# Sparse attention with a threshold search: new guess and steps, measures over two items, a fourth buffer

## The reference

```python
scores = einsum('bhqd,bhkd->bhqk', qh, kh) * scale
attn = sparsemax(scores)          # clip(scores - tau, 0), tau such that each row sums to 1
out = einsum('bhqk,bhkd->bhqd', attn, vh)
```

## Time and profile before

| | us |
|---|---|
| median of 3 runs (6928.72 to 6942.44) | 6930.95 |
| the profiled execution | 6886.64 |
| its span | 6884.8 |
| DVE busy in the span | 6013.5 |
| ACT busy in the span | 5560.1 |
| PE busy in the span | 5091.3 |
| POOL busy in the span | 2476.3 |

### The profile page before, as it was taken

One profiled execution on the slowest core, in us unless ns is written; L12 is line 12 of the kernel. 1 busy time (PEld: TensorE's weight loads), 2 busy tenths in 40 slices (PEclk: granted clock), 3 DMA queues, 4 the chain that ended last, 5 costly groups with the idle time before them and its releaser, 6 DMA issues. The chain is left out here.

```text
span 6884.8 us, 164804 instructions
## 1 busy us (share of the span) xinstructions
PE 5091.3 (74%) x19554; PEld 1665.0 (24%) x19555; DVE 6013.5 (87%) x50066; ACT 5560.1 (81%) x12484; POOL 2476.3 (36%) x10299
## 2 busy tenths in 40 slices
PE   8985777776777777676777777777777777758794
PEld 5551111111111111111111111111111111127573
DVE  4558999999999999999999999999999999958545
ACT  3336998998999999898999999998999999953231
POOL 2222333333333333333333333333333333325431
PEclk9996676766676666666666666666766766778897
DMA  5762111111111111111111111111111111136335
GB/s 195 238 200 59 30 33 30 31 33 30 31 32 32 31 31 32 28 31 27 31 31 32 31 31 31 32 31 29 34 32 32 31 33 34 31 126 240 96 100 192
DMA packets 691616, 415.98 MB, mean 60 GB/s; under 512 B 503713, under 2 KB 597537, under 8 KB 690209
## 3 DMA queue, kind: packets, MB, share of 16 engines
q1 hardware_dynamic: 677408, 370.58, 21.6%
q0 software_dynamic: 13056, 35.74, 1.4%
HBM read 249.13 MB, written 156.88 MB: 59 GB/s over the span
## 5 line engine op out<-in xcount | busy, mean ns | idle before, releaser
L887 DVE MAX8 a_cand<-a_scores 128x8 f32<-128x42 f32 (+1 forms) x38912 | 4400.3, 202 | 176.7 <-issue 136.7
L633 ACT ACTIVATE a_junk_act<-a_cand,a_ntau 128x304 f32<-128x304 f32 (+1 forms) x3840 | 1933.4, 522 | 143.6 <-POOL a_ntau L964 50.4
L603 PE MATMUL a_ring<-a_q,a_k 99*128 99x512 bf16 (+1 forms) x3328 | 1469.9, 556 | 735.2 <-ACT a_scores L669 509.2
L548 PE MATMUL a_out<-a_attn,a_v 128*32 128x512 f32 (+1 forms) x6656 | 1401.4, 780 | 543.5 <-ACT a_attn L673 543.5
L669 ACT COPY a_scores<-a_ring 128x1024 f32<-128x1024 f32 (+1 forms) x2048 | 1611.2, 830 | 152.3 <-PE a_ring L599 83.9
L673 ACT ACTIVATE a_attn<-a_ring 128x1024 f32<-128x1024 f32 (+1 forms) x1792 | 1654.2, 975 | 54.4 <-PE a_ring L603 53.3
L599 PE MATMUL a_ring<-a_k,a_q 96*128 96x512 bf16 (+1 forms) x4096 | 1368.7, 464 | 69.7 <-DVE a_ident L700 33.7
L633 ACT ACTIVATION_READ_ACCUMULATOR a_junk_act<-a_cand,a_ntau 128x1 f32 x3840 | 797.6, 208 | 0.0
L599 PEld LDWEIGHTS a_ring<-a_k,a_q 96*128 96x128 bf16 x4096 | 389.8, 117 | 1423.2 <-issue 645.6
L603 PEld LDWEIGHTS a_ring<-a_q,a_k 99*128 99x128 bf16 (+1 forms) x3328 | 287.8, 119 | 1583.2 <-ACT a_scores L669 890.0
L548 PEld LDWEIGHTS a_out<-a_attn,a_v 128*32 128x32 f32 (+1 forms) x6656 | 172.5, 121 | 1200.8 <-ACT a_attn L673 745.5
(11 more groups left out here) (228 smaller groups left out, 6364.8 us busy)
## 6 DMA issues: line engine op xcount, KB each, us to landing
a_k<-k_parts SPq DMA_DIRECT2D x1536, 50.0 KB
k_parts<-p_ks SPq DMA_DIRECT2D x48, 800.5 KB, 7.3
o_parts<-a_o SPq DMA_DIRECT2D x512, 64.0 KB, 1.6
e_o<-o_parts SPq DMA_DIRECT2D x64, 512.0 KB, 7.4
p_ctx<-in_ctx_t SPq DMA_DIRECT2D x16, 1601.0 KB, 8.5
v_heads<-p_v SPq DMA_DIRECT2D x16, 1536.0 KB
a_q<-q_parts SPq DMA_DIRECT2D x1536, 16.0 KB
a_v<-v_heads SPq DMA_DIRECT2D x256, 96.0 KB
```

Source lines behind the costliest of these rows:

```text
L548: mm = nc.tensor.matmul(out_ps[at:at + 2 * HEAD_DIM], beside, attn[0:rows, k, (c % 2) * BANK:(c % 2 + 1) * BANK], start=first and c < 4, s ...
L603: mm = nc.tensor.matmul(at[0:rows, m * BANK:(m + 1) * BANK], k_st[0:SCORE_ROWS + TAU_ROWS, ut, c * P:c * P + rows], q_st[0:SCORE_ROWS + TA ...
L633: ins = nc.scalar.activation(into[:, t].rearrange("p (a b) -> p a b", b=CHUNKS), cand[:, u % SLOTS, t, 0:w], ACT.Relu, bias=ntau[:, u % 2, ...
L887: ins = V.max(cand[:, u % SLOTS, t, :, c], scores[:, u % SLOTS, t, lo:hi])
```

## The change

- **Guess.** DVE's `start` makes `bn_stats` (means and spreads) of the chunks' greatest scores instead, adds the two halves' spreads, and reduces the eighth candidates. POOL's new `guess` makes tau and a model of how tau falls with the excess from these, with one `pow` for a square root. The sums, the counts and their reciprocals are gone from DVE.
- **Round 0** reads six candidates of each chunk (228 per row) instead of four.
- **Steps.** POOL's `first`, then `factors` and `improve` for each of two further steps, replace `second`, `third` and `slope`. Each `factors` needs a reciprocal that DVE makes in `inverse`: one beside t3, one beside t0.
- **Places.** On ACT in step i: after the first group round 2 of item i-2, then round 0 of item i-1, round 3 of item i-2, round 1 of item i-1. DVE's part of round 3 moves from t0 to t2. POOL's order becomes `improve` 1 of item i-2, `guess(i-1)`, `factors` and `improve` 2 of item i-2, `divide_up(i-3)`, `first(i-1)`, `factors` 0 of item i-1, `last_step(i-2)`.
- **An item later.** `settle(i-3)` stands beside t1, `SLOTS` is 4 and `LAG` is 4.
- `BEFORE_LAST` is 4.5e-4 instead of 3e-4; `full_excess` combines its 128 flags with two maxima in place of four copies.

```diff
-FIRST, SECOND = 2, 4
-USUAL_COUNT = 22.0
+SECOND = 6
+GUESS_AT, GUESS_SPREAD = 0.0202, 6.42
+FALL_AT, FALL_SPREAD = 0.0035, 0.693
+NEAR = 0.03, 0.001
-BEFORE_LAST = 3e-4
+BEFORE_LAST = 4.5e-4
...
-    SLOTS = 3
+    SLOTS = 4
-    LAG = 3
+    LAG = 4
+    TAUS = 3
...
-                    if part == 2 and has(i, 2):
-                        count_bad(i - 2)
+                    if part == 0 and has(i, 3):
+                        count_bad(i - 3)
...
-                    if g == 0 and has(i, 2):
-                        measure_excess(i - 2, (u - 2) % U, ROUNDS - 1)
-                    if g > 0 and has(i, 1):
-                        measure_excess(i - 1, (u - 1) % U, g - 1)
+                    if g % 2 == 0 and has(i, 2):
+                        measure_excess(i - 2, (n - 2) % LONG, 2 + g // 2)
+                    if g % 2 == 1 and has(i, 1):
+                        measure_excess(i - 1, (n - 1) % LONG, g // 2)
...
+                c, st = cand[:, u % SLOTS], stats[:, u % 2]
+                for t in range(TILES):
+                    ins = V.bn_stats(st[:, t], c[:, t, 0])
                 yield from link(ins)
+                V.tensor_tensor(spread_sq[:, u % 2], st[:, :, 2], st[:, :, 5], ALU.add).then_inc(spread_made, 1)
+                V.tensor_reduce(tops[:, u % TAUS], c[:, :, 7], AX.X, ALU.max, negate=True)
+
+            def inverse(i, n):
+
+                dve.wait_ge(square_made[n], i + 1)
+                V.reciprocal(square_inv[:], square[:]).then_inc(inv_made[n], 1)
...
+                    if t == 0 and has(i, 1):
+
+                        dve.wait_ge(cand_made, i)
+                        yield from start(i - 1, prev, link)
                     if t == 0 and has(i, 2):
+                        for _ in range(4):
                             yield
+                        inverse(i - 2, 1)
+                    if t == 1 and has(i, 3):
+                        yield from settle(i - 3, done, link)
+                    if t == 2 and has(i, 2):
+                        yield
+                        dve.wait_ge(tau_tried[ROUNDS - 2], i - 1)
...
                     if t == 3 and has(i, 1):
+                        inverse(i - 1, 0)
...
+                def guess(i, u):
+
+                    st, nt = stats[:, u % 2], ntau[:, u % TAUS]
+                    pool.wait_ge(spread_made, i + 1)
                     pool.sem_inc(passed_pool, 1)
+                    G.tensor_tensor(center[:], st[:, :, 1], st[:, :, 4], ALU.add)
+                    link(G.tensor_scalar(near[:], spread_sq[:, u % 2], -GUESS_SPREAD / CHUNKS, GUESS_AT, ALU.mult, ALU.add))
+                    link(G.tensor_scalar(center[:], center[:], -0.5, None, ALU.mult))
+                    G.tensor_tensor(nt, center[:], near[:], ALU.add).then_inc(guessed, 1)
+                    link(G.tensor_tensor(spread[:], spread_sq[:, u % 2], halves[:], ALU.pow))
+                    G.tensor_scalar(fall0[:], spread[:], FALL_SPREAD / CHUNKS ** 0.5, FALL_AT, ALU.mult, ALU.add)
+
+                def first(i, u):
+
+                    nt = ntau[:, u % TAUS]
+                    pool.wait_ge(excess_made[0], i + 1)
                     pool.sem_inc(passed_pool, 1)
+                    link(G.tensor_scalar(over[:], excess[:, u % 2, 0], 2.0, -1.0, ALU.min, ALU.add))
+                    link(G.tensor_scalar(bend[:], over[:], -0.5, 1.0, ALU.mult, ALU.add))
+                    link(G.tensor_tensor(rise[:], over[:], bend[:], ALU.mult))
+                    link(G.tensor_tensor(move[:], rise[:], fall0[:], ALU.mult))
+                    G.tensor_tensor(nt, nt, move[:], ALU.subtract).then_inc(tau_tried[0], 1)
+                    link(G.tensor_tensor(square[:], rise[:], rise[:], ALU.mult))
+                    G.tensor_scalar(square[:], square[:], NEAR[0] ** 2, None, ALU.add).then_inc(square_made[0], 1)
+
+                def factors(i, u, n, fall, rise):
+
+                    G.tensor_scalar(half[:], fall, -0.5, None, ALU.mult)
+                    pool.wait_ge(inv_made[n], i + 1)
                     pool.sem_inc(passed_pool, 1)
+                    link(G.tensor_tensor(share[:], rise, square_inv[:], ALU.mult))
+                    link(G.tensor_tensor(linear[:], share[:], fall, ALU.mult))
+                    link(G.tensor_tensor(cubic[:], linear[:], share[:], ALU.mult))
+                    G.tensor_tensor(linear_b[:, n], linear[:], half[:], ALU.add)
+                    G.tensor_tensor(cubic_b[:, n], cubic[:], linear[:], ALU.subtract)
+
+                def improve(i, u, r, fall, next_fall, over):
+
+                    nt = ntau[:, u % TAUS]
+                    pool.wait_ge(excess_made[r], i + 1)
                     pool.sem_inc(passed_pool, 1)
+                    link(G.tensor_scalar(over[:], excess[:, u % 2, r], 1.5, -1.0, ALU.min, ALU.add))
+                    link(G.tensor_tensor(term[:], over[:], cubic_b[:, r - 1], ALU.mult))
+                    link(G.tensor_tensor(term[:], term[:], linear_b[:, r - 1], ALU.add))
+                    link(G.tensor_tensor(term[:], term[:], over[:], ALU.mult))
+                    link(G.tensor_tensor(next_fall, term[:], fall, ALU.add))
+                    link(G.tensor_tensor(move[:], over[:], next_fall, ALU.mult))
+                    G.tensor_tensor(nt, nt, move[:], ALU.subtract).then_inc(tau_tried[r], 1)
...
+                prev, last = (u - 1) % LONG, (u - 2) % LONG
                 if has(i, 2):
+                    improve(i - 2, last, 1, fall0[:], fall1[:], over1)
+                    link(G.tensor_tensor(square[:], over1[:], over1[:], ALU.mult))
+                    G.tensor_scalar(square[:], square[:], NEAR[1] ** 2, None, ALU.add).then_inc(square_made[1], 1)
                 if has(i, 1):
+                    guess(i - 1, prev)
                 if has(i, 2):
+                    factors(i - 2, last, 1, fall1[:], over1[:])
+                    improve(i - 2, last, 2, fall1[:], fall2[:], over)
+                if has(i, 3):
+                    divide_up(i - 3, (u - 3) % LONG)
                 if has(i, 1):
+                    first(i - 1, prev)
+                    factors(i - 1, prev, 0, fall0[:], rise[:])
+                if has(i, 2):
+                    last_step(i - 2, last)
```

More of the change, by code:

```diff
@@ L433, in attend_program @@
         ones = sb("ones", [P, 1], BF16)
-        ntau = sb("ntau", [P, 2, TILES])
-        tops = sb("tops", [P, 2, 2, TILES])
+        ntau = sb("ntau", [P, TAUS, TILES])
+        tops = sb("tops", [P, TAUS, TILES])
         excess = sb("excess", [P, 2, ROUNDS, TILES])
[L438 to L444, removed]
+        stats = sb("stats", [P, 2, TILES, 6])
+        spread_sq, spread = sb("spread_sq", [P, 2, TILES]), sb("spread", [P, TILES])
+        halves = sb("halves", [P, TILES])
+        center, near = sb("center", [P, TILES]), sb("near", [P, TILES])
+        over, over1, bend, rise, move = (sb(n, [P, TILES]) for n in ("over", "over1", "bend", "rise", "move"))
+        square, square_inv, share = (sb(n, [P, TILES]) for n in ("square", "square_inv", "share"))
+        half, linear, cubic, term = (sb(n, [P, TILES]) for n in ("half", "linear", "cubic", "term"))
+        linear_b, cubic_b = sb("linear_b", [P, 2, TILES]), sb("cubic_b", [P, 2, TILES])
+        fall0, fall1, fall2 = (sb(n, [P, TILES]) for n in ("fall0", "fall1", "fall2"))
         cut_off, far_off = sb("cut_off", [P, TILES]), sb("far_off", [P, TILES])
-        e_bound = sb("e_bound", [P, TILES])
-        square = sb("square", [P, TILES])
-        fall = sb("fall", [P, TILES])
         bad = sb("bad", [P, TILES], BF16)
@@ L668, in step @@
                             t, lo, hi = S_PIECES[m]
-                            nc.scalar.copy(scores[:, u % SLOTS, t, lo:hi], at[:, 0:hi - lo]).then_inc(piece_used, 1)
+                            nc.scalar.copy(scores[:, n % SLOTS, t, lo:hi], at[:, 0:hi - lo]).then_inc(piece_used, 1)
                         else:
@@ L870, in beside @@
                         yield from start(i - 1, prev, link)
-                    if t == 2 and has(i, 2):
-                        yield from settle(i - 2, last, link)
+                    if t == 0 and has(i, 2):
+                        for _ in range(4):
[3 more added lines that the diff above has]
+                        yield from settle(i - 3, done, link)
+                    if t == 2 and has(i, 2):
+                        yield
+                        dve.wait_ge(tau_tried[ROUNDS - 2], i - 1)
+                        for n in range(ACT_LAST, TILES):
+                            values, nt = cand[:, last % SLOTS, n], ntau[:, last % TAUS]
+                            V.scalar_tensor_tensor(out=view(junk, values, CAND, n), in0=values, scalar=nt[:, n:n + 1], in1=zeros_like(values), op0=ALU.add, op1=ALU.max,
+                                                   accum_out=excess[:, last % 2, ROUNDS - 1, n:n + 1]).then_inc(last_summed, 1)
+                            yield
                     if t == 3 and has(i, 1):
-                        for _ in range(5):
```

(3 more changed lines are left out.)

173 lines of the change are left out of this document (46 added, 127 removed).

## The result

The changed kernel takes 7354.82 us (median of 4 runs, 7354.24 to 7361.58), the kernel before beside it 6936.32 (4 runs): ratio 1.0609, 95% interval 1.0596 to 1.0622. Slower, as forecast, but by 418 us instead of 56, outside the range of 6860 to 7090. The profiled execution took 7355.2 us with a span of 7353.3.

The account below looks back on a forecast made before the run. ACT was taken as the bound (97.8% busy in calm stretches), DVE just behind. Calm items +92, flags -41 and draining +5 gave +56 us on 6884.8, 0.8%, scaled to 6987 us; range 6860 to 7090, chance 0.8.

Parts of the forecast that it names:

- How many flags: Tiles sent to the whole-row pass: kept at 41, `cut_off` being unchanged; gain 41 x 1.0 = 41 us.
- floor of 36: Tiles with eight or more keys above tau in one chunk, counted from the reference's inputs: at least 36 stay flagged.
- The search is less exact: Rival on the search for tau: doubled flags cost 41 x 4.4 = 180 us more, 7167 us; chance 0.04.
- The price of a flag: Delay per tile needing the whole-row pass on DVE: 5.4 us before, 4.4 us after the change.
- absorbed: POOL's `divide_up(i-3)`, queued behind the whole-row pass, has 5 us until `first` must follow, so its delay costs nothing.
- The calm item: An item in a stretch without whole-row passes: 20.74 us before, 21.1 after, 0.36 x 256 = 92 us lost.
- term for the chain: From t3's copy over DVE and POOL to round 2: 7.4 us, with ACT's 13.75 a loop of 21.15 against 20.95.
- the wider round 0: ACT's round 0 goes from 152 to 228 elements per row: 0.06 us per tile, 0.25 us per item more.
- busy share: DVE's busy share of the span, 87% before, falls towards 85%; its work per item from 20.0 to 17.6 us.
- `pow`: POOL's square root in the guess: taken as 0.4 us; slow-`pow` rival, above 2.3 us DVE waits, 7090 to 7170, chance 0.12.
- The 5 us for the drain: `LAG` 4 adds a step of draining at the end, less what the first four steps lack: 5 us lost.

Follow-up runs that it names:

- `a_cutonly`: Changed kernel with the last measure's limit out of reach, so that only `cut_off` flags tiles: 7036.27 us, 36 flagged tiles.
- the reorder: Changed kernel with POOL's `last_step(i-2)` put ahead of `factors` 0: 7118.74 us; the same with no tile ever flagged: 6726.44 us.
- `a_divide`: Changed kernel with POOL's `divide_up(i-3)` put behind `first(i-1)`: 7362.4 us.
- `a_noflags`: Changed kernel with both limits out of reach, so that no tile is ever flagged: 6887.42 us.
- `b_noflags`: Kernel before, with both limits out of reach, so that no tile is ever flagged: 6705.71 us.

## Why the prediction went wrong

**The step that failed is "How many flags".** It kept 41, since `cut_off` is unchanged; that gives a floor of 36, and `a_cutonly` shows just 36. The runs count 71. For the tiles beyond the floor nothing in the trace of before speaks: how exact the new guess and steps are is arithmetic, and the prediction set its own rival "The search is less exact" at 0.04. 35 tiles missed by over the limit instead of five. Worked out on the reference's inputs, the excess sum misses 1 in the median by 0.034, 0.0004 and 0.000007 in the first three rounds of the old search, and by 0.064, 0.0035 and 0.00009 in the new: a poorer start and weaker steps. It takes the reference's inputs alone to see that, as for the floor of 36.

**The rival's price was also short.** It doubled the flags at 4.4 us and had no term for further steps: 25 instead of 4, 7.65 us each, cost more (161 us) than the 30 added tiles (117).

**The price of a flag** held: 4.4 us predicted against 5.4 before, 3.9 found against 4.6. That DVE's lag goes through the reciprocal to round 2 is borne out in part by the reorder: without flags it gains 161 us, with them 236, so 75 of the flags' 467 us hung on the length of that chain, and 392 stay with the shorter one. One detail fell: `divide_up` behind the settling was "absorbed" in the prediction, and ACT waited 219 us at `first`; yet `a_divide` takes that wait away, and the flags cost the same.

**The calm item** was forecast at +0.36 us and came at +0.72. Its term for the chain is the second step that failed. The windows of 2000 to 5000 us without flags, `a_noflags` and then `b_noflags` (ACT's busy time is the fourth of a window):

```profile
2000.00:5000.00 3000.00, 2288.09 (x8368) 497.12 (x8369) 2501.38 (x23016) 2872.29 (x6485) 1594.03 (x7394) 0.66 0.16 31
```
```profile
2000.00:5000.00 3000.00, 2270.89 (x8657) 520.28 (x8656) 2884.97 (x26697) 2927.57 (x6714) 1172.24 (x5625) 0.70 0.17 33
```

At 21.52 and 20.79 us these hold 139.4 and 144.3 items. ACT works 20.60 us per item against 20.29, 0.31 more where 0.25 were predicted for the wider round 0; the changed kernel's own 228-element tiles pass in 0.47 (3797.29 to 3797.76), as interpolated. It waits 60.4/139.4 = 0.43 us for L955, where the prediction had 0.15 for the chain. The chain's length and ACT's part were within 0.3 us, and away from the turns ACT waits (60.4 - 42)/139.4 = 0.13 us, close to the 0.15. The loop's turn, 3.6 us in the chain's middle once in twelve items, wasn't in it, and is the other 0.3. It cannot be read from an ordinary item of before, and the prediction read only one.

**The rest held.** DVE works 286.35 us in the 345 us from 3637 on, at 21.58 per item, so 17.9 per item against 17.6 predicted. Its busy share is 77% rather than 85; but the 85 doesn't follow from the prediction's own 2.4 us per item, which take 614 of 6013.5 us and leave 78% of the forecast span. `pow` is longer than assumed, 1.04 us against 0.4, and hidden as assumed up to 2.3. The 5 us for the drain don't show: 0.72 x 256 = 184 us of calm items are already the whole 182.

In sum, the 430 us are 117 + 161 - 29 for flags and 182 for calm items (431 by the rounded terms); the prediction had 0, 0, -41 and 97, the drain's 5 among it.

## What to carry to other kernels

Where a fallback path runs on data, ask first how often the change will take it, and work that out on the inputs: a cheaper estimate that misses more often is paid in the most costly branch. Where two engines and a handoff close a loop of about the length of the bound, add what happens once per turn of the unrolled loop, and keep work that nobody waits for out of the handoff: one `last_step` moved was worth 236 us. When a wait is taken away and the time stays, look at which wait took its place before taking away another.

## What the runs showed of the hardware

**The turn of a loop.** POOL's 3.54 us between two steps (above) is idle time without a releaser. In the DMA view of `a_noflags`, the queue's row for 3112.5 to 3116.5 us is

```profile
q14 instruction: 3, 0.02, 1.9%
```

and four equally long stretches elsewhere had one such packet between them. The Trainium skill (Runtime: NRT & Kernel Launch, section "Instruction fetch mechanics") says that a taken branch to a target outside the window that is loaded makes the engine fetch before it goes on. These rows agree with it, though the queue's row doesn't name the engine that fetched, and no run here shows it apart from other causes.

**POOL's operations.** `pow` and `bn_stats` in the changed kernel, 2000 to 5000 us, by form (busy us, mean ns | idle before):

```profile
L917 POOL TENSOR_TENSOR a_spread<-a_spread_sq,a_halves 128x4 f32<-128x4 f32 x129 | 133.9, 1038 | 0.0
...
L727 DVE BATCH_NORM_STATS2 a_stats<-a_cand 128x6 f32<-128x38 f32 x512 | 61.6, 186 | 0.0
```

A 128x4 `pow` takes 1.04 us, five times the 0.20 of the additions and products above; `bn_stats` over 38 elements 0.186 us, against 0.414 over 256.

**POOL beside a whole-row pass.** In the changed kernel, POOL's timeline during the pass at 629.49 (above) reads

```profile
629.20 0.20 POOL L951 TENSOR_TENSOR a_term<-a_term,a_linear_b 128x4 f32<-128x4 f32 x1 [0.18 <-POOL a_term L950]
629.58 1.85 POOL L952 TENSOR_TENSOR a_term<-a_term,a_over 128x4 f32<-128x4 f32 x1 [0.18 <-POOL a_term L951]
631.61 0.22 POOL L953 TENSOR_TENSOR a_fall<-a_term,a_fall 128x4 f32<-128x4 f32 x1 [0.18 <-POOL a_term L952]
```

An operation of 0.20 us stands for 1.85, until the pass has ended. The Trainium skill (SBUF — State Buffer, section "Who interferes with whom") says that a DVE instruction with two SBUF inputs contends with a GpSimd instruction that reads SBUF, and calls the shared pair of ports an exclusive lock. The rows agree: both of the pass's inputs, scores and zeros, stand in SBUF. The shorter `last_step` (2.49 us against 2.70), now beside MAX8, fits the same rule: 0.21 us less, where the prediction worked out 0.15. What the 1.65 us cost of each flag's time wasn't tried.
